# Local attention: six turns change places with neighbouring projections or PV halves in the order of a repeat

## The reference

```python
def attn_layer(x, Wqkv, qs, ksc, Wo):
    qkv = x @ Wqkv
    q, k, v = jnp.split(qkv, 3, -1)
    ...
    q = l2norm(q) * qs
    k = l2norm(k) * ksc
    ...                                   # rotary embedding of q and k
    out = local_attention(q, k, v)        # windows of 32, each looks at itself and the one before
    ...
    return out @ Wo
...
for i in range(DEPTH):                    # 6
    x = attn_layer(shift_tokens(x), Wqkv[i], q_scale[i], k_scale[i], Wo[i]) + x
    x = ffn_layer(shift_tokens(x), ln_g[i], ln_b[i], W1[i], b1[i], W2[i], b2[i]) + x
```

## Time and profile before

| | us |
|---|---|
| median of three runs | 4485.61 |
| lowest and highest | 4483.04, 4488.27 |
| profiled execution | 4482.78 |
| its span, first to last instruction | 4481.0 |
| TensorE matmuls busy in it | 4311.3 (96%) |
| VectorE busy | 3294.7 (74%) |
| ScalarE busy | 2639.2 (59%) |
| GpSimd busy | 2176.5 (49%) |

### The profile page before, as it was taken

The page is one execution under the profiler, slowest core; times in us unless marked ns, Lnnn a source line. Parts: engine busy times, 40 slices in busy tenths (PEclk is TensorE's granted clock), DMA queues, the critical chain, the costliest instruction groups (busy, mean ns, idle before and its releaser), DMA issues. The chain is left out here.

```text
span 4481.0 us, 172692 instructions
## 1 busy us (share of the span) xinstructions
PE 4311.3 (96%) x68832; PEld 2578.3 (58%) x68832; DVE 3294.7 (74%) x5792; ACT 2639.2 (59%) x5371; POOL 2176.5 (49%) x1993
## 2 busy tenths in 40 slices
PE   8999999998799999999999999999999999999998
PEld 4555555555466655665656665566656655556654
DVE  5666666666587877877877877787877877777875
ACT  4554555454466665666656665666656666666664
POOL 0000000000366766766766766666766766666763
PEclk9999999999899999999999999999999999999998
DMA  1000000000121112211121112211122111221112
GB/s 44 4 8 6 8 6 6 8 6 4 48 54 50 50 44 69 55 44 50 50 66 51 50 44 64 58 46 50 50 59 59 49 45 50 62 55 50 50 44 80
DMA packets 145061, 189.72 MB, mean 42 GB/s; under 512 B 34151, under 2 KB 66298, under 8 KB 144250
## 3 DMA queue, kind: packets, MB, share of 16 engines
q1 hardware_dynamic: 144250, 178.39, 14.7%
HBM read 29.39 MB, written 4.19 MB: 7 GB/s over the span
## 5 line engine op out<-in xcount | busy, mean ns | idle before, releaser
L1434 POOL TENSOR_TENSOR cs<-cs 128x512 f32<-128x512 f32 x768 | 975.9, 1276 | 569.3 <-DVE cs L1775 568.8
L1560 PE MATMUL psum<-wqkv,xw 128*128 128x512 f32 x2304 | 1187.4, 614 | 36.8 <-issue 19.5
L1775 DVE TENSOR_TENSOR cs<-psum,rots 128x1024 f32<-128x1024 f32 x768 | 938.2, 1222 | 277.1 <-PE psum L1560 268.9
L1443 POOL TENSOR_TENSOR qk<-cs,rn 128x512 f32<-128x512 f32 x768 | 776.6, 1043 | 430.3 <-ACT rn L1639 414.7
L1655 ACT ACTIVATE sq<-psum 128x512 f32<-128x512 f32 x768 | 458.7, 597 | 560.6 <-DVE cs L1775 539.4
L1467 POOL MEMSET tiled<- 128x128 bf16 x1 | 0.2, 204 | 1170.1 <-POOLq L524 1170.1
L1504 PEld LDWEIGHTS psum<-pT,vw 64*64 64x64 f32 x18624 | 405.8, 135 | 209.3 <-issue 208.7
L1729 DVE TENSOR_REDUCE ss<-sq 128x8 f32<-128x512 f32 x768 | 519.4, 676 | 6.9
L1560 PEld LDWEIGHTS psum<-wqkv,xw 128*128 128x128 f32 x2304 | 370.9, 191 | 200.7 <-issue 173.5
L1504 PE MATMUL psum<-pT,vw 64*64 64x32 f32 x18624 | 450.7, 221 | 24.5 <-issue 17.1
L1565 PEld LDWEIGHTS psum<-ident,qk 128*128 128x128 f32 x3088 | 358.5, 143 | 172.1 <-issue 164.7
(11 more groups left out here) (205 smaller groups left out, 6628.8 us busy)
## 6 DMA issues: line engine op xcount, KB each, us to landing
vw<-vl SPq DMA_DIRECT2D x768, 128.0 KB, 2.4
vw<-vl SPq DMA_DIRECT2D x672, 64.0 KB, 2.0
wqkv<-in_wqkv SPq DMA_DIRECT2D x42, 256.0 KB, 3.8
wol<-in_wol SPq DMA_DIRECT2D x7, 512.0 KB, 4.0
w1l<-in_w1l SPq DMA_DIRECT2D x7, 341.0 KB
xin<-in_x SPq DMA_DIRECT2D x9, 256.0 KB, 2.9
xr<-in_x SPq DMA_DIRECT2D x8, 256.0 KB, 2.9
sums<-sumout SPq DMA_DIRECT2D x8, 256.0 KB, 2.3
```

The lines of the kernel that those rows point to most:

```text
L1434: summed_rot.done(nc.gpsimd.tensor_tensor(own, own, halves(cs[:, t % 2, j, 1, :])[:, :, ::-1, :], ALU.add), at)
L1443: rotated.done(nc.gpsimd.tensor_tensor(qk[:, j, :].rearrange("p (h c) -> p h c", c=EL), cs[:, t % 2, j, 0, :].rearrange("p (h c) -> p h c" ...
L1560: last = nc.tensor.matmul(ps[:, :], xw[:, t * P:(t + 1) * P], wqkv[:, col:col + BANK], start=True, stop=True)
L1775: parts.done(V.tensor_tensor(cs[:, t % 2, j, :, :].rearrange("p i (h c) -> p i h c", c=EL), twice, by_head, ALU.mult), at)
```

## The change

Six exchanges of neighbours in `BODY`, nothing else; `OF_LAST` keeps its order. `pt.2.1` goes ahead of `v.0.0`, `t.0.0` ahead of `v.0.1`, `t.0.3` behind `oa.2`, `pt.3.0` ahead of `qk.1.3`, `pt.1.0` ahead of `qk.3.1`, and `pt.1.1` from its place ahead of `xn` to behind `sa.2`. In each case a turn then stands directly behind a segment where a projection stood before.

```diff
     qk.0.0 t.3.0 qk.0.1 t.3.1 t.3.2 t.3.3 qk.0.2 qk.0.3 n.0 y2.0 pt.2.0 qk.1.0 sa.3
-    v.0.0 pt.2.1 s.3.0 s.3.1 v.0.1 t.0.0 t.0.1 w.3 t.0.2 qk.1.1 t.0.3 oa.2
-    qk.1.2 o.2.0 o.2.1 qk.1.3 pt.3.0 sa.0 n.1 pt.3.1 v.1.0 s.0.0 s.0.1 qk.2.0
+    pt.2.1 v.0.0 s.3.0 s.3.1 t.0.0 v.0.1 t.0.1 w.3 t.0.2 qk.1.1 oa.2 t.0.3
+    qk.1.2 o.2.0 o.2.1 pt.3.0 qk.1.3 sa.0 n.1 pt.3.1 v.1.0 s.0.0 s.0.1 qk.2.0
     v.1.1 t.1.0 w.0 t.1.1 oa.3 t.1.2 qk.2.1 o.3.0 o.3.1 t.1.3 qk.2.2 pt.0.0
     qk.2.3 v.2.0 sa.1 pt.0.1 qk.3.0 s.1.0 s.1.1 n.2 w.1 y v.2.1 t.2.0
-    t.2.1 xt oa.0 t.2.2 t.2.3 o.0.0 o.0.1 qk.3.1 pt.1.0 pt.1.1 xn qk.3.2
-    qk.3.3 sa.2 v.3.0 v.3.1 s.2.0 s.2.1 n.3 gate.0 gate.1 w.2 up.0 gate.2 oa.1
+    t.2.1 xt oa.0 t.2.2 t.2.3 o.0.0 o.0.1 pt.1.0 qk.3.1 xn qk.3.2
+    qk.3.3 sa.2 pt.1.1 v.3.0 v.3.1 s.2.0 s.2.1 n.3 gate.0 gate.1 w.2 up.0 gate.2 oa.1
     up.1 up.2 o.1.0 o.1.1
```

## The result

The changed kernel takes 4507.51 us (median of 5 runs, 4504.40 to 4513.36) where the kernel before took 4488.27 us beside it: a ratio of 1.0049, 95% interval 1.0034 to 1.0063. Repeated in a later series it took 4512.17 us against 4483.74, a ratio of 1.0062 (1.0048 to 1.0076). So it is slower by 0.5 to 0.6%; the forecast was 4506.6 us, 0.47% slower. The profiled execution took 4511.21 us, 28.4 more than that of the kernel before, and the 48 repeats hold 27.0 us of this.

A forecast was written before the change was run, and what follows sets the result against it. TensorE was taken to set the end. Exchanges -13.0, oa.2 +25.0, t.1.1 +12.6 and breaks -3.6 gave +21.0 us on the 4485.6 median: 4506.6 us, 0.47% slower, range 4492 to 4520, chance 0.60.

The forecast's parts named there:

- What the exchanges give: TensorE behind segments: a projection pays 0.10 us, a turn 0.055; six exchanges save 0.045 each, 13.0 us in 48 repeats.
- oa.2's wait: oa.2 waits for ScalarE's copy of t.0.0 behind s.3's exponentials: 0.66 us in place of 0.14, +25.0 us.
- t.1.1's wait: t.1.1 waits for GpSimd's weighting because qk.1.3 completes later: 0.36 us in 35 of 48 repeats, +12.6 us.
- sa.2 without a wait: After the last two exchanges sa.2 keeps room 0.17 us against a reaction of 0.09: no wait, nothing charged.
- The breaks: Instruction-stream breaks in line L1504 (16.3 us) shorten behind a TensorE wait; a fifth estimated to go, -3.6 us.
- A clean repeat: Sign to look for: a repeat without a break takes 66.3 us after the change, 65.71 before.
- A: Rival: the waits come but L1504's breaks swallow them, +8.3 us, 4494 us; chance 0.13.
- B: Rival: oa.2 waits no longer than before, the 0.09 us behind the copy being chance; 4485 or 4472.6 us; chance 0.09.
- C: Rival: the tiling switch costs the same whatever follows, so exchanges save nothing; +34 us, 4520 us; chance 0.07.
- D: Rival: more breaks, or a wait at sa.2 in the repeat's second half; +14 us, 4520 us; chance 0.11.

The follow-up runs named there:

- the run with three exchanges: Kernel before with only pt.2.1 ahead of v.0.0, pt.1.0 ahead of qk.3.1 and pt.1.1 behind sa.2: 4473.60 us, ratio 0.9988.
- both causes gone: Changed kernel with qk.1.3 back ahead of pt.3.0 and ScalarE copying t.0.0 ahead of s.3's exponentials: 4467.16 us, ratio 0.9965; again 4470.24, 0.9959.
- the order with the covering projection: Changed kernel with qk.1.2 ahead of oa.2 and qk.1.3 ahead of pt.3.0, on all engines: 4487.84 us, ratio 1.0011 against the kernel before.

## Why the prediction was right, and which term was not

**What the exchanges give: -13.0 us forecast.** Right. t.0.0 and pt.2.1 take 0.49 behind a segment; the projections behind them take 0.86 (v.0.1) and, since a segment follows, 0.95 (v.0.0). The step sums of the five pairs without oa.2 are 2.1 to 2.3 us lower each, 10.9 in all; oa.2's own pair is part of the next term. The Trainium skill (TensorEngine Tiling (Array Packing), Key Properties) has the drain at a change of tiling mode but no price for what follows it; the trace has 0.10 for a projection and 0.055 for a turn, and the run with three exchanges was 5.4 us faster.

**oa.2's wait: +25.0 forecast.** Right, in size and in cause. The steps qk.1.1, t.0.3 and qk.1.2 together grew by 35.9 - 8.6 - 4.8 = 22.5 us; with the 2.1 of the exchange added back the wait cost 24.6. From qk.1.1 to oa.2 are 1.63 us, as forecast (1.6). One small thing was off: oa.2 starts 0.15 behind the end of this copy, not 0.09 as behind v.0.1's in the earlier trace rows. ScalarE's copy took 0.57, not 0.61, and that hid it.

**t.1.1's wait: +12.6 forecast.** Right. The step sum of t.1.0 grew by 11.9 us. The reaction was 0.15, so the full wait is 0.44 us, just above the upper of the bounds given (0.42) and not the 0.36 taken; and it is paid in fewer repeats. Where a break falls into s.0.0, t.1.0 takes 0.44 again, as the forecast had it; the waits view has 27 rows with an idle time long enough to be listed, where 35 were charged. Too many repeats and too small a wait nearly cancel, so that 12.6 came so close to 11.9 is in part luck.

**sa.2 without a wait.** Right: no idle time ahead, with 0.19 us between squaring and start.

**The breaks: -3.6 forecast, +2.6 in the trace.** This term had the wrong sign, and it was also mis-sized by its own rule: a fifth of 16.3 us is 3.3. In the step sums o.2.0 did get shorter, by 3.4 us. That a wait ahead shortened it is not shown, since the runs without any wait at oa.2 have o.2.0 shorter still (50.4 to 51.6 us against 54.7). And s.0.0 grew by 4.7, s.2.0 by 2.7 and o.3.0 by 2.0, while sa.2 lost 2.5. All steps together: -10.9 + 22.5 + 11.9 + 2.6 = +26.1 us in 47 repeats, 27.0 with the last one. The trace of the repetition has 4.7 us more in all steps, so there the term is larger and of the same sign. The first timing, +19, lies below this and the second, +28, above; the forecast of +21 owes part of its nearness to the first to the wrong sign, which is luck.

**A clean repeat: 66.3 us forecast.** Right: the one shown takes 66.38, and the 0.07 more is the wait for t.1.1, 0.43 there and not 0.36.

**The rivals.** A (breaks swallow the waits) is excluded by the traces: there are more breaks, not fewer. B fell with the run that only moved ScalarE's copy of v.0.1, C with the step lengths. Of D, more breaks did come: the term ended 6.2 us above the forecast's, where D had 14, and sa.2 did not wait.

## What to carry to other kernels

When a list sets the order of all engines, a step that is moved for TensorE's sake moves in every other engine's line too. Before moving it, ask which bank or tile the next waiting step takes, who frees it, and behind what that reader stands: an exchange that gains 0.045 us on TensorE cost 0.5 us through a copy that had not moved at all. Often the cheap cure is on the other engine; reading one copy ahead of two exponentials on ScalarE gave 15 us, and all six exchanges could give no more than 13.

## What the runs showed of the hardware

**Breaks end with an instruction packet.** I counted as a break every pause over 0.15 us between neighbouring product records (L1489, L1504) inside a segment: 64 in the kernel before (37.3 us) and 89 in the changed one (45.2 us; 79 and 44.3 in its repetition). That is more time than the "issue" lines of the waits view show, since a record's modelled length hides part of the pause. The trace's DMA records have a queue of instructions, with packets of 9.37 MB / 572 = 16 KB (from the page of the kernel before):

```profile
q8 instruction: 572, 9.37, 0.9%
```

In the changed kernel all 89 breaks end 1.21 to 1.62 us after one of these packets has landed; in the kernel before 63 of the 64 end 1.19 to 1.59 us after. In the 48 repeats of the kernel before the packets come 3.1 to 13.6 us apart, 6.1 in the median, and of all product records only 6% lie that far behind a packet, so this is no accident. The reading that fits is that in a segment TensorE runs out of instructions. That this queue is TensorE's is inferred from the match; the trace doesn't name its reader.

**With the wait at oa.2 gone, the breaks move, and fewer of them is not shown.** The five traces in which ScalarE's copy is early have o.2.0 at 50.4 to 51.6 us in the step sums, close to 50.1 for no break at all, while the eight in which oa.2 waits have 54.0 to 59.5. Between the kernel before (58.2) and the same order with the early copy (50.4) not one TensorE instruction differs. But s.0.0, two segments further on, goes the other way: 49.2 to 52.3 us in the five, 43.9 to 49.9 in the eight. The two together are 99.6 to 103.8 in the five and 98.9 to 105.7 in the eight, and the counted breaks of all segments are 35.1 to 46.0 us in the five and 34.6 to 45.2 in the eight. Two traces of one kernel already differ by 5 to 6 us in all steps (3184.8 and 3189.5 us for the changed kernel, 3139.6 and 3145.5 with both causes gone). So what a wait ahead of a segment costs beyond itself can't be read from these runs.

sa.2 is a second place where time moves. The exchange of pt.1.1 cuts its room from 0.59 us to 0.19 without making a wait. In all ten runs with this exchange s.2.0 sums to 40.4 to 44.0 us, in the three without it to 38.5, 38.6 and 38.9 (39.6 in the kernel before); but sa.2 itself is 2.5 us shorter in the changed kernel (49.3 for 51.8). The first half of the scores gets shorter and the second longer, and the two roughly cancel.

**What stays open.** That a waiting step holds TensorE's instruction queue, so that the next packet is asked for later, would explain the breaks behind oa.2. It is argued and not shown. It doesn't explain s.0.0, which grew where o.2.0 shrank; in the order before, the sum of the two fell by 3.3 us with the early copy. So of the 15 us that this copy gave, the 7 at t.0.3 have a cause and the rest has none that is shown. And the order with the covering projection had no wait at oa.2, 0.33 us of room, and the largest breaks in o.2.0 (62.6 us). Two PV halves with one turn between them stand closer together than elsewhere in the repeat. Whether this, or something else about the order, made the breaks of that run was not separated, and it doesn't reach s.0.0, which grew more.
